# First expert products of two chunks worked as a pair, the half-filled fifth matmuls as two 64-row tiles of the array

## The chip, the cores and the metric

The kernel runs on one core of a Trainium2 chip. The metric is the device time of one execution in microseconds (us); the time before is the median of three runs. A profile of one execution gives each instruction's start and duration. TensorE is called PE in its rows, its weight loads PEld, VectorE DVE, ScalarE ACT, GpSimd POOL and the queue that issues most DMAs SP.

## The reference

One block of a vision model on a map of 192 channels by 128 by 128 positions, in fp32. First a channel attention (1x1 convolution, 3x3 depthwise convolution, attention over channels, projection) with a residual. Then the part that is changed, a mixture of four experts over the 16384 positions as tokens:

```python
scores = jnp.einsum('bsd,de->bse', x, gate_w) + gate_b
probs = jax.nn.softmax(scores, axis=-1)
topk_vals, topk_idx = jax.lax.top_k(probs, TOP_K)          # TOP_K = 2 of 4 experts
...
h = jax.nn.gelu(jnp.einsum('bsd,edh->ebsh', x, w1) + b1[:, None, None, :], approximate=False)
y = jnp.einsum('ebsh,ehd->ebsd', h, w2) + b2[:, None, None, :]
out = jnp.einsum('bse,ebsd->bsd', masked, y)
```

A token has 192 numbers, the hidden layer of an expert 768.

## The kernel before

The first phase of the program (the `p1` block) does the normalisation, both convolutions and the products of the attention. The second (`p2`) projects, routes the tokens, and works the experts; at the end the result is transposed and written. All engines are programmed by hand, each with its own loop over "beats", and meet by semaphores. The order on every engine is therefore the order of the code.

Tokens that chose the same expert are scattered into lists in DRAM and read back in blocks of 512 (`TOK`). There are 67 blocks (`NJ`), one to a beat. A block has six chunks (`CH`) of 128 hidden units, so there are 402 chunks. Within a beat, for block `J` and chunk `k`:

- PE, `first(J, k)`: the hidden units of chunk `k` for 512 tokens, into one of the two banks `lb`, bank `k % 2`.
- ACT, `chunk`: Gelu out of the bank into `hf`, then a rounded copy `hh`. DVE: the rest, `hl = hf - hh`.
- PE, `second(J, k - LAG)`, two chunks later (`LAG` is 2): four token tiles of 128, each one matmul with `hh` (384 columns) and one with `hl` (192 columns), summed over the chunks in the four banks `yb`. The last two chunks of a block are worked in the next beat.
- PE, `turn`: eight transposes bring the next block's tokens (`xs`) into two banks `mb`; ACT and DVE split them into high and low parts. Every few beats `project` follows at the end of the beat (16 matmuls), for the stage before the experts.
- DVE, `expert_out(J)`: for each of the four tiles `upper` (first half of the bank times the gate weight, plus bias) and `lower` (second half added). `second(J, 0)` may overwrite tile `t` of `yb` when `lower(t)` of the block before is done. POOL then adds the tile to DRAM with an indirect DMA.

Accuracy is kept by splitting each factor into a rounded high part and a low rest, held as fp32r. A token has 192 numbers where the array has 128 rows. So `first` takes three full matmuls for the first 128 numbers (high x high, low weights x high, high weights x low), and for the last 64 the two halves of the rows are used for two things: `x_c` holds the high parts in rows 0 to 63 and the low parts in rows 64 to 127. The fourth matmul (weights quarter 2, the high weights in both halves) gives high x high and high x low at once. The fifth (quarter 3, the low weights in both halves) is needed only for low weights x high parts, that is for half of its rows.

## Time and profile before

| what | value |
|---|---|
| time, median of 3 runs (lowest, highest) | 1994.67 us (1994.42, 1999.99) |
| span of the profiled execution | 1993.4 us |
| the execution's time beside its span | not given apart; the median lies 1.3 us above the span |
| TensorE busy in the span | 1838.7 us (92%) |
| VectorE, ScalarE, GpSimd busy | 1379.8 (69%), 1277.2 (64%), 1123.5 (56%) |
| DMA, mean over the span | 182 GB/s |
| first matmul of the experts, last one of `second` | 834 us, 1906 us |

The span goes from the first to the last instruction. A busy time is the union of an engine's instructions; those of TensorE overlap, since a matmul's recorded duration reaches to its last result while the next one is already streaming. What a matmul takes of the engine is the distance from its start to the next start.

### The profile page before, as it was taken

To read this page: it belongs to the slowest core of one execution; us is meant where nothing else is said; L and a number is where in the kernel's file an instruction comes from. 1 tells how busy PE (TensorE), PEld (TensorE's weight loads), DVE (VectorE), ACT (ScalarE), POOL (GpSimd) and SP (SyncE) were. 2 spreads that over 40 slices of the span, in tenths; PEclk is the share of its full clock that TensorE was granted. 3 is DMA by queue.
4 is the path that set the end of the run, shared out by engine and by line. 5 is a ranking of instruction groups with operands and counts; after the bars stand their busy time and mean duration, and the time that the engine had idled before them with its cause. 6 is when DMAs were issued, how large, how long until landed. Compare 5 with 4: busy or idle time off the path is not lost.

```text
span 1993.4 us, 36026 instructions
## 1 busy us (share of the span) xinstructions
PE 1838.7 (92%) x9782; PEld 1502.9 (75%) x9782; DVE 1379.8 (69%) x3382; ACT 1277.2 (64%) x2468; POOL 1123.5 (56%) x1079
## 2 busy tenths in 40 slices
PE   5799999999795989898999999999999999999956
PEld 3566666666564767688989989899898888888844
DVE  3789999999777474667676686776766655555532
ACT  3688888888674435465666666666667667676622
POOL 3666666666663015476767676767677676344320
PEclk9899999999896999899999999999999999999977
DMA  3453323333333798777788878788787877656569
GB/s 97 147 148 93 92 89 93 92 91 92 99 111 95 228 290 275 263 221 216 211 229 215 227 213 228 213 229 224 216 226 195 242 204 202 171 155 180 129 184 338
DMA packets 254367, 361.97 MB, mean 182 GB/s; under 512 B 27396, under 2 KB 183940, under 8 KB 254212
## 3 DMA queue, kind: packets, MB, share of 16 engines
q1 hardware_dynamic: 191556, 278.59, 46.3%
q0 software_dynamic: 50880, 60.59, 15.0%
q10 hardware_dynamic: 11776, 20.98, 3.0%
q8 instruction: 67, 1.10, 0.2%
q14 instruction: 88, 0.72, 0.1%
HBM read 222.76 MB, written 137.30 MB: 181 GB/s over the span
## 4 chain that ended last, share of the span: by engine, by line
PE 57%; DMA 4%; DVE 3%; POOL 2%; issue 2%; ACT 1%; SPq 1%; POOLq 0%; DVEq 0%; ACTq 0%
PE bank L1804 21%; PE bank L1820 14%; PE bank L1787 7%; PE bank L1821 6%; PE bank L1847 4%; DMA xn<-acc_scratch 3%; PE bank L1839 3%; POOL xs_scratch L1251 1%; POOL acc_scratch L1266 1%; PE bank L1869 1%; DMA acc_scratch<-yo,tix 1%; DMA xs<-xs_scratch 0%; PE bank L1872 0%; DVE hl L1758 0%; ACT L1319 0%
## 5 line engine op out<-in xcount | busy, mean ns | idle before, releaser
L1266 POOL DMA_INDIRECT acc_scratch<-yo,tix x268 | 439.0, 1638 | 304.2 <-DVE yo L1647 238.0
L1804 PE MATMUL bank<-x_all,w1b 128*128 128x512 f32 x2010 | 548.8, 402 | 1.0 <-ACT hf L1319 1.0
L1820 PE MATMUL bank<-w_hl,hh 128*128 x1608 | 495.5, 360 | 6.7 <-DVE hl L1758 5.8
L1319 ACT ACTIVATE hf<-bank,b_col 128x512 f32<-128x512 f32 x402 | 276.7, 688 | 335.5 <-PE bank L1804 335.4
L1758 DVE TENSOR_TENSOR hl<-hf,hh 128x512 fp32r<-128x512 f32 x402 | 277.2, 690 | 272.5 <-ACT hh L1322 272.3
L1821 PE MATMUL bank<-w_hl,hl 128*128 x1608 | 404.9, 252 | 0.0
L1804 PEld LDWEIGHTS bank<-x_all,w1b 128*128 128x128 f32 x2010 | 348.2, 188 | 55.1 <-ACT hf L1319 1.4
L625 DVE SCALAR_TENSOR_TENSOR bank<-zwin,wdw,bank 128x512 f32<-128x512 f32 (+2 forms) x462 | 336.3, 734 | 43.4 <-PE bank L731 34.8
L1820 PEld LDWEIGHTS bank<-w_hl,hh 128*128 128x128 f32 x1608 | 302.1, 188 | 40.9 <-issue 10.4
L1821 PEld LDWEIGHTS bank<-w_hl,hl 128*128 128x128 f32 x1608 | 306.1, 190 | 17.4
L1251 POOL DMA_INDIRECT xs_scratch<-xn,idx x256 | 262.2, 1024 | 85.1 <-issue 75.7
L1322 ACT ACTIVATE hh<-hf 128x512 fp32r<-128x512 f32 x402 | 253.9, 632 | 12.7
L429 POOL TENSOR_TENSOR last_tap<-acc,last_tap 128x512 f32<-128x512 f32 (+2 forms) x99 | 125.5, 1268 | 181.6 <-ACT last_tap L495 146.0
L731 PE MATMUL bank<-zwin,diag 128*128 128x512 f32 (+2 forms) x462 | 213.8, 592 | 3.4 <-DVE acc L625 3.4
L731 PEld LDWEIGHTS bank<-zwin,diag 128*128 128x128 f32 x462 | 83.6, 194 | 69.7 <-issue 61.1
L1787 PE MATMUL bank<-x_all,w1b 120*96 120x512 f32 x381 | 123.8, 423 | 6.7 <-issue 3.7
L432 POOL TENSOR_TENSOR qs<-last_tap,s_bc 128x512 f32<-128x512 f32 (+2 forms) x99 | 124.1, 1254 | 7.8
L1642 DVE SCALAR_TENSOR_TENSOR yo<-bank,wt,b2w 128x192 f32<-128x192 f32 x268 | 104.4, 410 | 30.1 <-PE bank L1821 30.0
L1329 ACT ACTIVATE b2w<-b2b,wt 128x192 f32 x268 | 118.1, 441 | 0.0
L1647 DVE SCALAR_TENSOR_TENSOR yo<-bank,wt,yo 128x192 f32<-128x192 f32 x268 | 103.7, 407 | 0.0
L1847 PE MATMUL bank<-mt,vd 96*128 96x200 f32 (+1 forms) x512 | 98.3, 346 | 5.7 <-DMA vd<-u_scratch 3.5
L479 ACT ACTIVATE zwin<-bank,bz 128x512 f32<-128x512 f32 x96 | 66.1, 688 | 58.4 <-PE bank L773 58.4
(261 smaller groups left out, 2902.3 us busy)
## 6 DMA issues: line engine op xcount, KB each, us to landing
w1b<-w1s_scratch SPq DMA_DIRECT2D x134, 768.0 KB, 5.1
xs<-xs_scratch SPq DMA_DIRECT2D x67, 522.0 KB, 6.0
xtok_scratch<-xtok SPq DMA_DIRECT2D x32, 384.0 KB, 2.7
v_scratch<-zv SPq DMA_DIRECT2D x64, 192.0 KB
vc_scratch<-yo ACTq DMA_DIRECT2D x64, 192.0 KB, 4.5
vd<-vc_scratch SPq DMA_DIRECT2D x64, 192.0 KB
xtok<-xtok_scratch SPq DMA_DIRECT2D x32, 384.0 KB, 7.3
acc_scratch<-x SPq DMA_DIRECT2D x32, 384.0 KB, 5.5
```

What stands on the lines that cost most here:

```text
L625: nc.vector.scalar_tensor_tensor(out=acc[:, ct, lo:hi, :] if last else bank, in0=zwin[n.par][:, ct, ky + lo:ky + hi, kx:kx + W], scalar=wd ...
L731: last = nc.tensor.matmul(db[(n.par + ct) % 2][:, lo * W:hi * W].rearrange("p (r w) -> p r w", w=W), diag[:, ct, k, :], zwin[n.par][:, ct, ...
L1251: nc.gpsimd.indirect_dma_start(xs_dram, bass.IndirectOffsetOnAxis(ap=idx[:, h, b * NT + t:b * NT + t + 1], axis=0), src, None).then_inc(st ...
L1266: nc.gpsimd.indirect_dma_start(acc_dram, bass.IndirectOffsetOnAxis(ap=tix[:, J % 4, t:t + 1], axis=0), yo[:, J % YN, t, :], None, compute_ ...
L1319: nc.scalar.activation(hf[:, k % 3, :], lb[k % 2][:, :], ACT.Gelu, bias=b1_col[:, bass.ds(exp_of[J] * CH + k, 1)]).then_inc(gelu, 1)
L1322: nc.scalar.activation(hh[:, k % 3, :], hf[:, k % 3, :], ACT.Copy).then_inc(hh_ok, 1)
L1758: nc.vector.tensor_tensor(hl[:, k % 3, :], hf[:, k % 3, :], hh[:, k % 3, :].bitcast(FP32), ALU.subtract).then_inc(hl_ok, 1)
L1787: last = nc.tensor.matmul(cb[u % 4][0:MV, :].rearrange("p (b w) -> p b w", w=W), w[:, kx, :], v[:, :, kx:kx + W], start=(n == 0), stop=(n ...
L1804: last = nc.tensor.matmul(lb[k % 2][:, :], w[:, q, :], v[:, J % 2, :], start=(i == 0), stop=(i == 4))
L1820: nc.tensor.matmul(yb[t][:, 0:2 * C], hh[:, k % 3, cols], w, start=(k == 0), stop=False, skip_group_check=True)
L1821: last = nc.tensor.matmul(yb[t][:, 0:C], hl[:, k % 3, cols], w[:, 0:C], start=False, stop=(k == CH - 1), skip_group_check=True)
L1847: last = nc.tensor.matmul(mb[t // 2][:, t % 2 * CY:t % 2 * CY + CY], vd[0:rows, s % 2, g, t, :], mt[0:rows, g, :], start=(g == 0 and t % 2 ...
```

## The change

In `first_pair(J, k)` the chunks `k` and `k + 1` are worked together, `k` even. Bank 0 gets the four whole matmuls of chunk `k`, then its fifth as a matmul of 64 rows (rows 0 to 63 of the array). Directly behind it comes the fifth of chunk `k + 1` as a matmul of rows 64 to 127, into bank 1, which it opens, and then the four whole ones of chunk `k + 1`. The 64-row matmuls read a new tile `xh_c`, which holds the high parts in both halves. It costs ACT one more copy per block (x_c's upper 64 rows), since `x_c` can't hold both.

Two `second`s follow each pair. The transposes of the next block come after `second(J, 1)` and no longer after `second(J, 0)`; ACT and DVE split them one chunk later. The second half of a block's weights is waited for before chunk 2 and not before chunk 3. `expert_out` is in two halves: tiles 0 and 1 before `hl` of chunk 1, tiles 2 and 3 behind it. Some small tiles are made smaller or share a place, to make room for `xh_c`.

```diff
@@ scalar
-                        if k == 2 and nxt is not None:
+                        if k == 3 and nxt is not None:
...
                             act.wait_ge(ac2, 2 * nxt + 2)
-                            nc.scalar.activation(x_c[:, nxt % 2, :], mb[1][:, :], ACT.Copy).then_inc(hi2, 1)
+                            nc.scalar.activation(xh_c[:, nxt % 2, :], mb[1][:, :], ACT.Copy).then_inc(hi2, 1)
+                            nc.scalar.activation(x_c[0:CB, nxt % 2, :], mb[1][0:CB, :], ACT.Copy).then_inc(hi2, 1)
@@ vector
-                    upper(0)
-                    for t in range(1, ROWS):
+                    for t in tiles:
                         upper(t)
-                        lower(t - 1)
-                    lower(ROWS - 1)
+                    for t in tiles:
+                        lower(t)
...
                         if k == 1 and prev is not None:
-                            expert_out(prev)
-                        if k == 3 and nxt is not None:
+                            expert_out(prev, (0, 1))
+                        if k == 4 and nxt is not None:
...
                             nc.vector.tensor_tensor(hl[:, k % 3, :], hf[:, k % 3, :], hh[:, k % 3, :].bitcast(FP32), ALU.subtract).then_inc(hl_ok, 1)
+                        if k == 1 and prev is not None:
+                            expert_out(prev, (2, 3))
@@ tensor
-                def first(J, k):
+                def first_pair(J, k):
...
-                    if k % 3 == 0:
-                        pe.wait_ge(ld_w1[J % 2][k // 3], 16 * (J // 2 + 1))
+                    if k != 4:
+                        pe.wait_ge(ld_w1[J % 2][k // 2], 16 * (J // 2 + 1))
                     wait(pe, gelu, c - 1)
-                    w = w1b[:, J % 2, k, 0:512].rearrange("p (q n) -> p q n", q=4)
-                    ops = [(0, xh_a), (1, xh_a), (0, xl_a), (2, x_c), (3, x_c)]
-                    for i, (q, v) in enumerate(ops):
-                        last = nc.tensor.matmul(lb[k % 2][:, :], w[:, q, :], v[:, J % 2, :], start=(i == 0), stop=(i == 4))
+                    w = w1b[:, J % 2, k:k + 2, 0:512].rearrange("p m (q n) -> p m q n", q=4)
+                    whole = [(0, xh_a), (1, xh_a), (0, xl_a), (2, x_c)]
+                    for i, (q, v) in enumerate(whole):
+                        nc.tensor.matmul(lb[0][:, :], w[:, 0, q, :], v[:, J % 2, :], start=(i == 0), stop=False)
+                    wait(pe, gelu, c)
+                    nc.tensor.matmul(lb[0][:, :], w[0:CB, 0, 3, :], xh_c[0:CB, J % 2, :], start=False, stop=True).then_inc(l1, 1)
+                    nc.tensor.matmul(lb[1][:, :], w[CB:128, 1, 3, :], xh_c[CB:128, J % 2, :], start=True, stop=False)
+                    for i, (q, v) in enumerate(whole):
+                        last = nc.tensor.matmul(lb[1][:, :], w[:, 1, q, :], v[:, J % 2, :], start=False, stop=(i == 3))
                     last.then_inc(l1, 1)
...
-                    for k in range(CH):
+                    for k in range(0, CH, 2):
                         if J is not None:
-                            first(J, k)
-                        if k < LAG:
-                            if prev is not None:
-                                second(prev, CH - LAG + k)
-                        elif J is not None:
-                            second(J, k - LAG)
+                            first_pair(J, k)
+                        for m in (k, k + 1):
+                            if m < LAG:
+                                if prev is not None:
+                                    second(prev, CH - LAG + m)
+                            elif J is not None:
+                                second(J, m - LAG)
                         if k == 2 and nxt is not None:
                             turn(nxt, n)
```

The order on TensorE from chunk 2's `first` into `second(J, 0)`, before. L1804 is `first`, L1812 reads the block's expert, L1820 and L1821 are the `hh` and `hl` matmuls of `second`:

```order
L1804 MATMUL bank<-x_all,w1b 128x512 x5
L1812 TENSOR_LOAD tab
L1812 ISA x2
L1820 ISA
L1820 MATMUL bank<-w_hl,hh 128x384
L1821 MATMUL bank<-w_hl,hl 128x192
```

The same place after the change. L1805 and L1810 are the whole matmuls of the two chunks, L1807 and L1808 the two of 64 rows (the shape shown is that of the result), L1826 and L1827 stand for `second`:

```order
L1805 MATMUL bank<-x_all,w1b 128x512 x4
L1807 MATMUL bank<-x_all,w1b 128x512
L1808 MATMUL bank<-x_all,w1b 128x512
L1810 MATMUL bank<-x_all,w1b 128x512 x4
L1818 TENSOR_LOAD tab
L1818 ISA x2
L1826 ISA
L1826 MATMUL bank<-w_hl,hh 128x384
L1827 MATMUL bank<-w_hl,hl 128x192
```

The number of matmuls is the same, ten for two chunks. They now stand in one stretch, with the two of 64 rows in its middle, and two `second`s (each four times the last two rows) stand behind one another.

On VectorE, `expert_out` of the block before (L1642 `upper`, L1647 `lower`) among the `hl` of the chunks (L1758), before:

```order
L1758 TENSOR_TENSOR hl<-hf,hh 128x512 x4
L1642 SCALAR_TENSOR_TENSOR yo<-bank,wt,b2w 128x192 x2
L1647 SCALAR_TENSOR_TENSOR yo<-bank,wt,yo 128x192
L1642 SCALAR_TENSOR_TENSOR yo<-bank,wt,b2w 128x192
L1647 SCALAR_TENSOR_TENSOR yo<-bank,wt,yo 128x192
L1642 SCALAR_TENSOR_TENSOR yo<-bank,wt,b2w 128x192
L1647 SCALAR_TENSOR_TENSOR yo<-bank,wt,yo 128x192 x2
L1758 TENSOR_TENSOR hl<-hf,hh 128x512 x2
```

And after, where `hl` is L1757:

```order
L1757 TENSOR_TENSOR hl<-hf,hh 128x512 x3
L1642 SCALAR_TENSOR_TENSOR yo<-bank,wt,b2w 128x192 x2
L1647 SCALAR_TENSOR_TENSOR yo<-bank,wt,yo 128x192 x2
L1757 TENSOR_TENSOR hl<-hf,hh 128x512
L1642 SCALAR_TENSOR_TENSOR yo<-bank,wt,b2w 128x192 x2
L1647 SCALAR_TENSOR_TENSOR yo<-bank,wt,yo 128x192 x2
L1757 TENSOR_TENSOR hl<-hf,hh 128x512 x2
```

The eight operations of `expert_out` are the same; one `hl` now stands between the two halves.

## Rows read from the trace of the kernel before

**Rows 1.** The page's chain that ended last, by engine and by line

```profile
PE 57%; DMA 4%; DVE 3%; POOL 2%; issue 2%; ACT 1%; SPq 1%; POOLq 0%; DVEq 0%; ACTq 0%
PE bank L1804 21%; PE bank L1820 14%; PE bank L1787 7%; PE bank L1821 6%; PE bank L1847 4%; DMA xn<-acc_scratch 3%; PE bank L1839 3%; POOL xs_scratch L1251 1%; POOL acc_scratch L1266 1%; PE bank L1869 1%; DMA acc_scratch<-yo,tix 1%; DMA xs<-xs_scratch 0%; PE bank L1872 0%; DVE hl L1758 0%; ACT L1319 0%
```

**Rows 2.** Busy times by stretch, experts in the second row

```profile
core 0: us, PE busy (x) PEld busy (x) DVE busy (x) ACT busy (x) POOL busy (x), PEclk, DMA share, GB/s
906.00:1906.00 1000.00, 995.80 (x5741) 896.21 (x5740) 656.75 (x1767) 672.46 (x1185) 634.48 (x482) 1.00 0.77 204
```

**Rows 3.** Groups by line, whole span, two of TensorE

```profile
L1804 PE MATMUL bank<-x_all,w1b 128*128 128x512 f32 x2010 | 548.8, 402 | 1.0 <-ACT hf L1319 1.0
L1820 PE MATMUL bank<-w_hl,hh 128*128 x1608 | 495.5, 360 | 6.7 <-DVE hl L1758 5.8
```

**Rows 4.** Timeline of TensorE, a beat's chunks: start, us, what

```profile
1206.45 1.35 PE L1804 MATMUL bank<-x_all,w1b 128*128 128x512 f32 x5
1207.64 0.34 PE L1820 MATMUL bank<-w_hl,hh 128*128 x1
...
1208.76 1.34 PE L1804 MATMUL bank<-x_all,w1b 128*128 128x512 f32 x5
1209.94 0.34 PE L1820 MATMUL bank<-w_hl,hh 128*128 x1
...
1210.20 0.36 PE L1820 MATMUL bank<-w_hl,hh 128*128 x1
1210.40 0.25 PE L1821 MATMUL bank<-w_hl,hl 128*128 x1
1210.59 0.44 PE L1820 MATMUL bank<-w_hl,hh 128*128 x1
1210.87 0.25 PE L1821 MATMUL bank<-w_hl,hl 128*128 x1
```

**Rows 5.** Timeline of TensorE and its weight loads at the first phase's setup

```profile
23.03 0.42 PE L847 MATMUL bank<-ident,wpr 128*96 128x128 f32 x1
23.38 0.34 PE L848 MATMUL bank<-ident,wpr 64*96 64x64 f32 x1
...
22.82 0.20 PEld L847 LDWEIGHTS bank<-ident,wpr 128*96 128x96 f32 x1
23.38 0.15 PEld L848 LDWEIGHTS bank<-ident,wpr 64*96 64x96 f32 x1 [0.36 <-issue]
```

**Rows 6.** Timeline of TensorE around three matmuls of 3 rows, and its clock there

```profile
630.65 3.19 PE L1787 MATMUL bank<-x_all,w1b 120*96 120x512 f32 x7
...
633.21 0.63 PE L1787 MATMUL bank<-x_all,w1b 120*96 120x512 f32 x1
633.77 0.52 PE L1888 MATMUL bank<-rn_row,sel 3*96 3x128 f32 x1
...
633.77 1.59 PE L1888 MATMUL bank<-rn_row,sel 3*96 3x128 f32 x6
...
634.94 0.42 PE L1888 MATMUL bank<-rn_row,sel 3*96 3x128 f32 x1
635.29 0.74 PE L1787 MATMUL bank<-x_all,w1b 120*96 120x512 f32 x1
...
630.00:637.00 7.00, 7.00 (x19) 4.49 (x19) 3.22 (x10) 1.10 (x3) 0.00 (x0) 0.50 0.37 105
```

**Rows 7.** Who waited for whom, 906 to 1900 us: total, times, longest

```profile
ACT hf L1319 <- PE bank L1804: 318.3, 356, 9.8
DVE hl L1758 <- ACT hh L1322: 253.4, 249, 2.5
...
PEld bank L1820 <- DVE yo L1647: 9.1, 52, 0.3
```

**Rows 8.** Timeline of VectorE and ScalarE in the same beat as rows 4

```profile
1208.17 0.74 DVE L1642 SCALAR_TENSOR_TENSOR yo<-bank,wt,b2w 128x192 f32<-128x192 f32 x2 [0.46 <-PE bank L1821]
...
1210.13 0.73 DVE L1647 SCALAR_TENSOR_TENSOR yo<-bank,wt,yo 128x192 f32<-128x192 f32 x2
1210.78 0.68 DVE L1758 TENSOR_TENSOR hl<-hf,hh 128x512 fp32r<-128x512 f32 x1
...
1210.96 0.63 ACT L1322 ACTIVATE hh<-hf 128x512 fp32r<-128x512 f32 x1
1211.50 0.44 ACT L1329 ACTIVATE b2w<-b2b,wt 128x192 f32 x1
1211.93 0.60 ACT L1375 ACTIVATE x_all<-bank 128x512 fp32r<-128x512 f32 x1
1212.42 0.59 ACT L1377 ACTIVATE x_all<-bank 128x512 fp32r<-128x512 f32 x1
1213.64 0.69 ACT L1319 ACTIVATE hf<-bank,b_col 128x512 f32<-128x512 f32 x1 [0.62 <-PE bank L1804]
```

**Rows 9.** `project` on TensorE: a timeline row, and the group by line

```profile
1201.43 2.90 PE L1847 MATMUL bank<-mt,vd 96*128 96x200 f32 x16
...
L1847 PE MATMUL bank<-mt,vd 96*128 96x200 f32 (+1 forms) x300 | 54.5, 334 | 0.0
```

More of the change, by code:

```diff
@@ L941, in build @@
             rcol = sb(p2, "rcol", [128, 8, NT])
-            tri = sb(p2, "tri", [128, NT, E, E])
+            tri = sb(p2, "tri", [128, E, E])
             msk = sb(p2, "msk", [128, NT, E])
@@ L953, in build @@
             tokid = sb(p2, "tokid", [128, NB * ROWS])
-            tok_i = sb(p2, "tok_i", [128, NB * ROWS], mybir.dt.int32)
+            tok_i = idx[:, 0, :].bitcast(mybir.dt.int32)
             tab = sb(p2, "tab", [128, NG, 2, MAXB], mybir.dt.int32)
@@ L974, in build @@
             xs = sb(p2, "xs", [128, 2, ROWS, CW])
-            x_all = sb(p2, "x_all", [128, 3, 2, TOK], F32R)
-            xh_a, xl_a, x_c = (x_all[:, k, :, :] for k in range(3))
-            zl_c = sb(p2, "zl_c", [128, 4, W + 2], F32R)
+            x_all = sb(p2, "x_all", [128, 4, 2, TOK], F32R)
+            xh_a, xl_a, x_c, xh_c = (x_all[:, k, :, :] for k in range(4))
             hf = sb(p2, "hf", [128, 3, TOK])
@@ L1006, in build @@
             z_hi = [window(x_all, n * ZW, KV, 4, W + 2) for n in range(3)]
-            z_lo = [window(x_all, (3 + n) * ZW, KV, 4, W + 2) for n in range(2)] + [zl_c[0:KV, :, :]]
+            z_lo = [window(x_all, (3 + n) * ZW, KV, 4, W + 2) for n in range(2)] + [window(x_all, 6 * TOK, KV, 4, W + 2)]
             band_place = [(w1b, n * BW) for n in range(21)] + [(t, n * BW) for t in (hh, hl) for n in range(5)] + [(x_all, 5 * ZW)]
@@ L1217, in _ @@
                 nc.gpsimd.memset(zrow[:, :, :], 0.0).then_inc(c2, 1)
-                nc.gpsimd.memset(tri[:, :, :, :], 1.0).then_inc(c2, 1)
+                nc.gpsimd.memset(tri[:, :, :], 1.0).then_inc(c2, 1)
                 nc.gpsimd.memset(tri_s[:, :], 1.0).then_inc(c2, 1)
@@ L1228, in _ @@
                 pool.wait_ge(c2, 11)
-                nc.gpsimd.affine_select(out=tri[:, :, :, :], in_=tri[:, :, :, :], compare_op=ALU.is_gt, fill=0.0,
-                                        base=0, pattern=[[0, NT], [1, E], [-1, E]], channel_multiplier=0).then_inc(c2, 1)
+                nc.gpsimd.affine_select(out=tri[:, :, :], in_=tri[:, :, :], compare_op=ALU.is_gt, fill=0.0,
+                                        base=0, pattern=[[1, E], [-1, E]], channel_multiplier=0).then_inc(c2, 1)
                 nc.gpsimd.affine_select(out=tri_s[:, :], in_=tri_s[:, :], compare_op=ALU.is_gt, fill=0.0,
@@ L1487, in gate @@
                     linked()
-                    link(nc.vector.tensor_tensor(cmp_[:, 2], cmp_[:, 1], tri[:, :, :, :], ALU.mult))
+                    link(nc.vector.tensor_tensor(cmp_[:, 2], cmp_[:, 1], tri[:, None, :, :].to_broadcast([128, NT, E, E]), ALU.mult))
                     yield
@@ L1630, in meta, with expert_out @@
                     nc.vector.tensor_copy(tix[:, J % 4, :], xs[:, J % 2, :, CID]).then_inc(meta_ok, 1)
-                def expert_out(J):
-                    if J >= YN:
+                def expert_out(J, tiles):
+                    if tiles[0] == 0 and J >= YN:
                         added(dve, J - YN)
-                    if J == 0:
+                    if J == 0 and tiles[0] == 0:
                         stored(dve, UNITS)
@@ L1744, in _ @@
                         if k == 1 and prev is not None:
-                            expert_out(prev)
-                        if k == 3 and nxt is not None:
+                            expert_out(prev, (0, 1))
+                        if k == 4 and nxt is not None:
                             if J is None:
                                 some(places, 99)
-                            dve.wait_ge(hi2, 2 * nxt + 2)
+                            dve.wait_ge(hi2, 3 * nxt + 3)
                             nc.vector.tensor_tensor(xl_a[:, nxt % 2, :], mb[0][:, :], xh_a[:, nxt % 2, :].bitcast(FP32), ALU.subtract).then_inc(lo2, 1)
-                            nc.vector.tensor_tensor(x_c[CB:128, nxt % 2, :], mb[1][CB:128, :], x_c[CB:128, nxt % 2, :].bitcast(FP32), ALU.subtract)\
+                            nc.vector.tensor_tensor(x_c[CB:128, nxt % 2, :], mb[1][CB:128, :], xh_c[CB:128, nxt % 2, :].bitcast(FP32), ALU.subtract)\
                                 .then_inc(lo2, 1)
```

## The prediction

> **What bounds the kernel now.** I began with the chain that ended last [rows 1]: 57% of the span is TensorE's, and the lines of the experts (L1804, L1820, L1821, L1839) make up most of that. The busy times by stretch then say how tight this stage is [rows 2]: in 1000 us of the experts TensorE is busy for 995.80, at a granted clock of 1.00, while VectorE has 656.75, ScalarE 672.46 and GpSimd 634.48. The waits confirm it [rows 7]: ScalarE waited 318.3 us for the results of `first`, VectorE 253.4 us for ScalarE, and TensorE's only wait of size is 9.1 us in 52 places for `lower` (L1647), which frees the banks of `second`. So what TensorE spends from start to start in this stage is the time of the stage, and each microsecond added to or taken from it counts nearly whole.
>
> From start to start, five matmuls of `first` take 1207.64 - 1206.45 = 1.19 us and 1209.94 - 1208.76 = 1.18 us [rows 4]. One of 512 columns thus takes 0.24 us. The recorded mean of 402 ns [rows 3] is its latency and not its price.
>
> **The change part by part.** There are 67 blocks of six chunks, 402 chunks, 201 pairs; 2010 matmuls of `first` [rows 3] agree (402 x 5).
>
> *The fifth matmuls.* The two 64-row matmuls lie in different rows of the array and go to different banks. If they stream side by side, a pair saves one slot: 0.24 us, and 201 x 0.24 = 48 us in all. Against it stand two changes of the number of rows, 128 to 64 and back to 128, in each pair. The price of such a change is the whole question, and two places of this trace show it.
>
> At the setup a matmul of 128 rows is followed by one of 64 [rows 5]. In a stream the next weights are loaded while the matmul before is at work: L847's load begins at 22.82, its matmul only at 23.03. The load of L848, the 64-row one, begins at 23.38, after 0.36 us of idle time that no other engine ended, and at the same moment as its own matmul. Neither the load ahead nor the overlap of two matmuls is there across the change.
>
> The second place gives sizes, at the half clock (0.50, 1.2 GHz) [rows 6]. Seven matmuls of 120 rows by 512 columns take 3.19 us, the last of them 0.63: (3.19 - 0.63) / 6 = 0.43 us from start to start. The last one starts at 633.21 and the first of 3 rows at 633.77, 0.56 us on: 0.13 more than the 0.43. On the way back, 634.94 to 635.29 is 0.35 us, where these matmuls otherwise take (1.59 - 0.42) / 5 = 0.23: 0.12 more. And the first matmul after it lasts 0.74 instead of 0.63, since its weights were not yet there: 0.11 more. One change costs 0.13 of draining and 0.11 of an uncovered load, 0.24 us.
>
> That is at the half clock, and the experts run at the full one. The uncovered load has a row there: where `second` had waited for VectorE, its matmul and its load began together at 1210.59, it lasted 0.44 instead of 0.36, and the next start came 0.28 later where 0.20 is usual (1210.20 to 1210.40) [rows 4]: 0.08 us. The draining has no row at the full clock. Its bounds are 0.065 (all of it cycles of the array, half of 0.13) and 0.13 (none of it). I take the middle, 0.10, so that a change costs 0.18 us, with 0.145 and 0.21 as bounds. The half-clock rows are for 3 rows and not for 64, but the setup shows the same signature for 64.
>
> A price of nothing for the change can't be read from these rows. Matmuls of 96 and of 100 rows do alternate in `project` without any such stop, (2.90 - 0.33) / 15 = 0.17 us from start to start [rows 9]. So not every change of the row count costs; one down to 64 did in rows 5.
>
> *The second tile behind the first.* Its load can't lie under a whole matmul as others do. It lies between nothing (it is loaded together with the first one's) and an uncovered 0.08. I take 0.04.
>
> The sum for a pair: 2 x 0.18 + 0.04 - 0.24 = +0.16 us, and 201 x 0.16 = +32 us. The bounds are 2 x 0.145 + 0 - 0.24 = +0.05 (+10 us) and 2 x 0.21 + 0.08 - 0.24 = +0.26 (+52 us).
>
> The Trainium skill (TensorEngine Tiling, section Key Properties) says the same: a change of the tiling mode, not of the tile alone, drains TensorE. It gives no figure; the rows above do.
>
> *The stall at second(J, 0).* Before, `second(prev, 5)` and `second(J, 0)` are one `first` (1.18 us) apart, and the eight operations of `expert_out` run from 1208.17 to 1210.86 [rows 8], past the start of `second(J, 0)` at 1209.94 [rows 4]. Hence the 9.1 us in 52 waits [rows 7], to which 52 uncovered loads of 0.08 are to be added (4.2 us): 13 us. After the change the two are a whole pair apart, some 2.5 us. `lower` of tiles 2 and 3 then comes later by one `hl` of 0.68 us [rows 8], but is needed later by 1.3 us: `expert_out` starts 0.53 us after `second(prev, 5)` (1208.17, 1207.64), so tile 3 is ready 0.53 + 2.69 + 0.68 = 3.9 us after that start, and its bank is asked for at 1.12 + 2.5 + 3 x 0.28 = 4.5. The stall goes: -13 us. If it stays, nothing.
>
> *Waits that the new order brings.* Bank 0 is asked for at the start of a pair, bank 1 after four matmuls. Bank 1's chunk ended with the pair before, so Gelu has two `second`s (2 x 1.12) and four matmuls (0.95) for it, 3.2 us, where it needs 0.69, and at worst 0.63 of `hh` and 0.44 of a bias copy ahead of it [rows 8]. ScalarE has one more copy per block, at most 0.59 us as L1377's [rows 8]; the three copies follow the transposes, and the next Gelu (chunk 4) is due some 1.2 us after these end. So it may be late by about 0.6 us, but bank 0 is asked for again only in the next beat. The cover is ScalarE's idle share, a third of the stage [rows 2]; without it 67 x 0.6 = 40 us would show. `hl` of the pair's second chunk is needed after a full pair and one `second`, later than before in relation to its `first`. VectorE's splitting of the next block comes one chunk later and ends some 1.5 us ahead of the next beat. The weights' second half is asked for one chunk earlier; it is issued a beat ahead. All of these I cost at nothing. SP's queue keeps its order, and GpSimd's adds follow `lower`, for which POOL waits anyway.
>
> The small tiles of the setup (`tri`, `tok_i`) work on fewer elements or the same, outside the experts: nothing.
>
> Sum: +32 - 13 = +19 us. The profiled span is 1993.4 us and the median 1994.67, 1.3 us above it; the sum is made on the span, and the same 1.3 us lie around it afterwards: 1993.4 + 19 + 1.3 = 2014 us.
>
> **The rivals.**
>
> *The change of rows is cheap at the full clock, and the kernel gets faster.* If TensorE loads the 64-row weights ahead and only drains, at the lower bound, a pair costs 2 x 0.065 - 0.24 = -0.11 us: -22 us, with the stall -35, 1960 us. With no price at all it is -48 - 13 = -61 us, 1934 us. It decides below a price of about 0.13 us a change (2 x 0.13 + 0.04 - 0.24 = +0.06, 12 us, which the stall pays). For it: the half clock may exaggerate, and rows 9 show changes of row count for free. Against it: both places with a small row count show drain and uncovered load, and the uncovered load alone is 0.08 at the full clock. The rule that speaks for it is in the Trainium skill (TensorE: Matmul & The Clock Gate, Part 3): matmuls in different row tiles start about 4 ns apart, and a weight load for other rows overlaps a matmul in flight. Nothing in this trace shows two tiles at work. 13% for 1960, 4% for 1934.
>
> *The two tiles don't stream side by side.* Then the slot is not saved and both switches are paid: 0.24 in place of the 0.04, 201 x 0.20 = 40 us more, 2054 us. For it: the trace has no case of it, and both are fed from one queue in order. Against: different rows, different banks. 15%.
>
> *It cancels.* Both changes at the lower bound, +10, and the stall's -13, give -3 us: 1992 us, no change that a measurement tells (0.3%, 6 us, is what can be told here). 12%.
>
> **How the numbers follow.** The forecast, a real price at the full clock and tiles side by side, has 56%; its own range is 1994.7 + 10 - 13 = 1992 to 1994.7 + 52 = 2047. Slower by over 0.3% holds most of it and the case without overlap: 0.56 + 0.15, less a little at the lower edge, 0.70. Within 0.3%: 0.12. Faster by over 0.3%: 0.17, with the edge 0.18. The range reaches down between the forecast and the cheap switch, to 1976, and up to the case without overlap, 2056.
>
> **What would show it.** In the profile after: the start of the first 64-row matmul should lie about 0.33 to 0.37 us after the last whole one of bank 0 (0.24 in a stream), its weight load beginning with it and not before; the two 64-row starts should be 0.0 to 0.1 us apart (0.24 would mean no overlap); and the first whole one of bank 1 should come 0.3 us or more after them, again with its load uncovered. From the start of a pair to the first matmul of `second` it should be about 2.53 us where twice 1.185 is 2.37. The row of waits for L1647 should be gone. The prediction is wrong if the load of the 64-row weights begins under the whole matmul, if the pair takes under 2.3 us, or if TensorE's idle time in the experts grows, which would point to a wait (for Gelu, or for the split of the next block) and not to the array.

## The result and the profile after

| | time, median | runs | ratio to before (95% interval) |
|---|---|---|---|
| before | 1995.17 us | 6 | |
| after | 2005.25 us | 6 | 1.0046 (1.0032 to 1.006) |

The change makes the kernel 0.46% slower, some 9 to 10 us. Forecast were 19 us more (2014); the measured time lies in the range and has the sign of the forecast, but half its size. The span went from 1993.4 to 2003.5 us.

The busy times by stretch after (columns as in [rows 2]) still show a stage that TensorE fills:

```profile
906.00:1916.00 1010.00, 1009.41 (x5730) 844.18 (x5728) 654.07 (x1758) 682.75 (x1247) 646.77 (x480) 1.00 0.76 201
```

TensorE is now busy for all but 0.6 of 1010 us; before 4.2 of 1000 were idle [rows 2]. Its weight loads (PEld) fell from 896.21 us in 1000 to 844.18 us in 1010: they stand still where the row count changes. The price of that is in the timeline of TensorE, one pair of chunks:

```profile
1208.92 1.10 PE L1805 MATMUL bank<-x_all,w1b 128*128 128x512 f32 x4
1209.95 0.50 PE L1807 MATMUL bank<-x_all,w1b 64*128 64x512 f32 x1
1209.96 0.50 PE L1808 MATMUL bank<-x_all,w1b 64*128 64x512 f32 x1
1210.38 1.19 PE L1810 MATMUL bank<-x_all,w1b 128*128 128x512 f32 x4
1211.42 0.34 PE L1826 MATMUL bank<-w_hl,hh 128*128 x1
```

Its weight loads in the same place:

```profile
1209.95 0.18 PEld L1807 LDWEIGHTS bank<-x_all,w1b 64*128 64x128 f32 x1 [0.35 <-issue]
1209.95 0.18 PEld L1808 LDWEIGHTS bank<-x_all,w1b 64*128 64x128 f32 x1
1210.38 0.76 PEld L1810 LDWEIGHTS bank<-x_all,w1b 128*128 128x128 f32 x4 [0.25 <-issue]
```

The two 64-row matmuls start 0.01 us apart, so they do stream side by side. Their loads begin with them and not under the matmul before, after 0.35 us in which nothing was loaded: the signature of [rows 5]. The pair takes 1211.42 - 1208.92 = 2.50 us where twice 1.185 had been 2.37 (forecast 2.53).

So the signs named in the prediction came: load with the matmul and not before it, tiles side by side, and a gap of 0.43 us to the first whole matmul of bank 1 (1209.95 to 1210.38). The gap from the last whole matmul of bank 0 to the first 64-row one is 0.32 us in the middle of the 200 pairs of this trace, just under the 0.33 to 0.37 forecast.

The three largest waits of TensorE's weight loads in the experts, after (total, times, longest). `PEld ... <- issue` is no other engine's doing:

```profile
PEld bank L1807 <- issue: 71.5, 199, 0.4
PEld bank L1810 <- issue: 48.7, 200, 0.2
PEld bank L1826 <- issue: 4.1, 1, 4.1
```

The wait for `lower` in [rows 7] (9.1 us, 52 times) has no row any more. Of the waits that the new order might have brought, for Gelu before bank 1 (L1807), there is 0.4 us once in the whole stage.

### The profile page after: what moved, and what is told of

The parts are those of the page before. It is cut to its first block, busy times and chain, and to the rows that moved or that the text cites. A ratio compares the mean times of both kernels' runs of the same rounds, so it can differ in the third digit from the quotient of the medians.

```text
span 2003.5 us, 36093 instructions
## 1 busy us (share of the span) xinstructions
PE 1854.7 (93%) x9782; PEld 1449.9 (72%) x9782; DVE 1377.4 (69%) x3382; ACT 1289.4 (64%) x2535; POOL 1137.7 (57%) x1079
## 4 chain that ended last, share of the span: by engine, by line
PE 58%; DMA 4%; DVE 3%; POOL 2%; issue 2%; ACT 1%; SPq 0%; POOLq 0%; DVEq 0%; ACTq 0%
PE bank L1826 14%; PE bank L1810 10%; PE bank L1805 9%; PE bank L1788 7%; PE bank L1827 6%; PE bank L1853 4%; PE bank L1807 4%; DMA xn<-acc_scratch 3%; PE bank L1845 3%; POOL xs_scratch L1250 1%; POOL acc_scratch L1265 1%; DMA acc_scratch<-yo,tix 0%; PE bank L1875 0%; DVE hl L1757 0%; DVE stat L1436 0%
## 5 line engine op out<-in xcount | busy, mean ns | idle before, releaser
L1265 POOL DMA_INDIRECT acc_scratch<-yo,tix x268 | 449.0, 1675 | 300.8 <-DVE yo L1647 216.1
L1826 PE MATMUL bank<-w_hl,hh 128*128 x1608 | 473.2, 359 | 3.9 <-DVE hl L1757 3.9
L1757 DVE TENSOR_TENSOR hl<-hf,hh 128x512 fp32r<-128x512 f32 x402 | 277.3, 690 | 237.3 <-ACT hh L1321 236.9
L1827 PE MATMUL bank<-w_hl,hl 128*128 x1608 | 403.5, 251 | 0.0
L1827 PEld LDWEIGHTS bank<-w_hl,hl 128*128 128x128 f32 x1608 | 307.2, 191 | 8.9
L1826 PEld LDWEIGHTS bank<-w_hl,hh 128*128 128x128 f32 x1608 | 302.7, 188 | 13.3 <-issue 4.1
L1810 PE MATMUL bank<-x_all,w1b 128*128 128x512 f32 x804 | 241.8, 422 | 0.0
L1805 PE MATMUL bank<-x_all,w1b 128*128 128x512 f32 x804 | 229.0, 406 | 1.1 <-ACT hf L1318 1.1
L1810 PEld LDWEIGHTS bank<-x_all,w1b 128*128 128x128 f32 x804 | 135.3, 188 | 67.9 <-issue 48.9
L1805 PEld LDWEIGHTS bank<-x_all,w1b 128*128 128x128 f32 x804 | 137.0, 189 | 18.4 <-issue 1.5
L1788 PE MATMUL bank<-x_all,w1b 120*96 120x512 f32 x444 | 134.7, 413 | 7.7 <-issue 4.5
L1642 DVE SCALAR_TENSOR_TENSOR yo<-bank,wt,b2w 128x192 f32<-128x192 f32 x268 | 99.0, 410 | 27.9 <-PE bank L1827 27.6
```

The source lines that it names most:

```text
L1265: nc.gpsimd.indirect_dma_start(acc_dram, bass.IndirectOffsetOnAxis(ap=tix[:, J % 4, t:t + 1], axis=0), yo[:, J % YN, t, :], None, compute_ ...
L1757: nc.vector.tensor_tensor(hl[:, k % 3, :], hf[:, k % 3, :], hh[:, k % 3, :].bitcast(FP32), ALU.subtract).then_inc(hl_ok, 1)
L1788: last = nc.tensor.matmul(cb[u % 4][0:MV, :].rearrange("p (b w) -> p b w", w=W), w[:, kx, :], v[:, :, kx:kx + W], start=(n == 0), stop=(n ...
L1805: nc.tensor.matmul(lb[0][:, :], w[:, 0, q, :], v[:, J % 2, :], start=(i == 0), stop=False)
L1810: last = nc.tensor.matmul(lb[1][:, :], w[:, 1, q, :], v[:, J % 2, :], start=False, stop=(i == 3))
L1826: nc.tensor.matmul(yb[t][:, 0:2 * C], hh[:, k % 3, cols], w, start=(k == 0), stop=False, skip_group_check=True)
```

## The experiments

Each ratio is to the kernel before, timed beside that run, with its 95% interval. The "stage" is the time from the first start of `first` to the last start of an `hh` matmul of `second`, read from those two lines' rows. It leaves out the phases around it, which vary by a few us from run to run. The time of a part of the stage is summed from start to next start over the trace's matmuls. A "quiet beat" is one without `project` and without routing, from the first transposing matmul to the next beat's.

### Whole matmuls in the place of the tiles (e1)

```diff
-                    nc.tensor.matmul(lb[0][:, :], w[0:CB, 0, 3, :], xh_c[0:CB, J % 2, :], start=False, stop=True).then_inc(l1, 1)
-                    nc.tensor.matmul(lb[1][:, :], w[CB:128, 1, 3, :], xh_c[CB:128, J % 2, :], start=True, stop=False)
+                    nc.tensor.matmul(lb[0][:, :], w[:, 0, 3, :], x_c[:, J % 2, :], start=False, stop=True).then_inc(l1, 1)
+                    nc.tensor.matmul(lb[1][:, :], w[:, 1, 3, :], x_c[:, J % 2, :], start=True, stop=False)
```

> The changed kernel with its two 64-row matmuls made into whole ones of 128 rows again (reading x_c), in the same places; all else of the change stays, the pair order, the later split and the third copy on ScalarE too. The price theory reads from the profile after the change that a pair pays 0.158 us net for the tiles (from the last whole matmul of bank 0 to the second whole one of bank 1 it is 0.319 + 0.003 + 0.428 + 0.340 = 1.090 us where four slots are 0.932). It expects 201 x 0.158 = 32 us less than the changed kernel: about 1973 us, so 22 us under the kernel before. The rival, that what the order gave back hangs on the tiles or that a faster TensorE runs into a wait (a bank of Gelu, the banks of the second products), expects 1985 to 1995 us.

Measured: 1971.99 us, ratio 0.9882 (0.9864 to 0.99). The tiles cost 33 us, and what is left of the change gains 24. The price theory holds on the total. The pair itself shows more than it expected:

```profile
1212.29 1.10 PE L1805 MATMUL bank<-x_all,w1b 128*128 128x512 f32 x4
1213.22 0.39 PE L1807 MATMUL bank<-x_all,w1b 128*128 128x512 f32 x1
1213.45 0.39 PE L1808 MATMUL bank<-x_all,w1b 128*128 128x512 f32 x1
1213.68 1.07 PE L1810 MATMUL bank<-x_all,w1b 128*128 128x512 f32 x4
1214.58 0.34 PE L1826 MATMUL bank<-w_hl,hh 128*128 x1
```

Ten whole matmuls take 1214.58 - 1212.29 = 2.29 us, where the changed kernel's pair took 2.50. That is 0.20 us a pair, and some 38 to 40 us over 201 pairs, not 32. The stage grew by 33.2 us only (1050.1 to 1083.3), because waits behind the pairs shrink when TensorE is slower: the row `PE bank L1865 <- DVE x_all L1750: 2.5, 5, 0.7` of e1 (routing) has no counterpart after the change, and the one wait for `hl` at the start of the stage is 3.9 us in place of 5.3.

### Both 64-row matmuls in rows 0 to 63 (e2)

```diff
-                    nc.tensor.matmul(lb[1][:, :], w[CB:128, 1, 3, :], xh_c[CB:128, J % 2, :], start=True, stop=False)
+                    nc.tensor.matmul(lb[1][:, :], w[0:CB, 1, 3, :], xh_c[0:CB, J % 2, :], start=True, stop=False)
```

> The changed kernel with both 64-row matmuls in rows 0 to 63 of the array, so that they can't stream side by side; the number of changes between 128 and 64 rows stays. If the tiles do overlap in the changed kernel (starts 3 ns apart), and this is worth a slot, this one is 201 x 0.23 = 46 us slower than the changed kernel, about 2051 us. If in addition the second one's weights can't be loaded under the first, it is 0.1 us a pair more, about 2071 us. If the 3 ns are only how the starts are recorded, it takes the same 2005 us.

Measured: 2048.67 us, ratio 1.0263 (1.0246 to 1.028), 43 us more than the changed kernel. Its timeline of TensorE:

```profile
1210.93 1.18 PE L1805 MATMUL bank<-x_all,w1b 128*128 128x512 f32 x4
1212.04 0.49 PE L1807 MATMUL bank<-x_all,w1b 64*128 64x512 f32 x1
1212.37 0.39 PE L1808 MATMUL bank<-x_all,w1b 64*128 64x512 f32 x1
1212.70 1.20 PE L1810 MATMUL bank<-x_all,w1b 128*128 128x512 f32 x4
1213.73 0.34 PE L1826 MATMUL bank<-w_hl,hh 128*128 x1
```

From the first 64-row start to the first whole one it is 0.66 us, with tiles side by side 0.43. The overlap is real and worth a whole slot (the time from one start to the next in a stream, 0.23 us). The rival without overlap (15%) is out.

### The 64-row fifth in the old order (e3)

```diff
-                        last = nc.tensor.matmul(lb[k % 2][:, :], w[:, q, :], v[:, J % 2, :], start=(i == 0), stop=(i == 4))
+                        r = slice(0, CB if i == 4 else 128)
+                        last = nc.tensor.matmul(lb[k % 2][:, :], w[r, q, :], v[r, J % 2, :], start=(i == 0), stop=(i == 4))
```

> The kernel before, in its old order, with the fifth matmul of every chunk on rows 0 to 63 alone (it leaves out the product of the two low parts, which is negligible). Two changes of row count for each of 402 chunks and no second tile. The price theory expects per chunk 0.319 + 0.428 + 0.340 - 3 x 0.233 = 0.39 us, for the half that is followed by a wider second product rather less at its end, so between 402 x 0.3 and 402 x 0.39: 2115 to 2151 us. The rival, that the cost in the changed kernel comes from the change of bank or from two tiles loaded together, expects 1995 us.

Measured: 2117.35 us, ratio 1.0617 (1.0595 to 1.0639), 122 us over the kernel before: the lower end of the 2115 to 2151 expected. Five matmuls now take from 1212.10 to 1213.56, and the first of `second` behind them has its load uncovered (0.45 in place of 0.34, next start 0.28 later):

```profile
1212.10 1.53 PE L1805 MATMUL bank<-x_all,w1b 128*128 128x512 f32 x5
1213.56 0.45 PE L1821 MATMUL bank<-w_hl,hh 128*128 x1
1213.84 0.25 PE L1822 MATMUL bank<-w_hl,hl 128*128 x1
```

1213.84 - 1212.10 = 1.74 us where [rows 4] have 1207.82 - 1206.45 = 1.37 (the start of the `hl` matmul at 1207.82 is 0.18 behind 1207.64). That is 0.37 us for two changes, 402 x 0.37 = 149 us. The stage grew by 125 us (832.1 to 2029.2, 1197.1). The 24 us between the two are about what the kernel before lost to waits that are gone or shorter here: 15.5 us at `second(J, 0)` (see e10), 3.8 for `msk`, and 5 for `hl` at the start of the stage. One matmul of 64 rows among whole ones, in one bank and with no tile beside it, is enough for the price.

### The split of the next block at its old place (e4)

The transposes stand behind `second(J, 0)`, ScalarE's copies in chunk 2, VectorE's split in chunk 3; the fifths are whole.

```diff
-                        if k == 3 and nxt is not None:
+                        if k == 2 and nxt is not None:
                             act.wait_ge(ac2, 2 * nxt + 1)
...
-                        if k == 4 and nxt is not None:
+                        if k == 3 and nxt is not None:
...
-                        if k == 2 and nxt is not None:
-                            turn(nxt, n)
+                            if m == 2 and nxt is not None:
+                                turn(nxt, n)
```

> As e1, with whole fifths in the pair order, but the transposes of the next block again right behind second(J, 0), ScalarE's copies in chunk 2 and VectorE's split in chunk 3, as in the kernel before. The theory that the later split freed VectorE for the routing in time (TensorE's wait of 1.08 us for msk at 1284.41 before the change has no counterpart after it) expects the gate beats to lose about 0.8 to 1.1 us each again, 7 of them: 6 to 8 us over e1. A rival, that the pair order and the halved expert_out did it, expects the same time as e1.

Measured: 1972.63 us, ratio 0.9885 (0.9868 to 0.9901), the same as e1. My theory of the later split falls: with the split at its old place the wait in the routing beats is not longer but gone from the rows of TensorE's matmuls, while the one at the start of the stage is 7.1 us in place of e1's 5.3.

### expert_out in one piece (e5)

```diff
-                    for t in tiles:
-                        upper(t)
-                    for t in tiles:
-                        lower(t)
+                    upper(0)
+                    for t in range(1, ROWS):
+                        upper(t)
+                        lower(t - 1)
+                    lower(ROWS - 1)
...
-                            expert_out(prev, (0, 1))
+                            expert_out(prev, (0, 1, 2, 3))
...
-                        if k == 1 and prev is not None:
-                            expert_out(prev, (2, 3))
```

> As e1 (pair order, whole fifths, 1972 us), but expert_out in one piece again, in the old order of its eight operations, ahead of hl of chunk 1. The theory that the pair order on TensorE alone frees the banks of the second products in time (a pair, now 2.36 us, lies between second(prev, 5) and second(J, 0)) expects the same as e1, 1972 us within 3. The rival, that the halved expert_out is what removed the wait, expects the 52 waits of 0.2 us back: 8 to 13 us more.

Measured: 1972.28 us, ratio 0.9878 (0.9863 to 0.9894). The same as e1.

### Only expert_out in two halves, old order (e6)

The kernel before with the change's `expert_out` and nothing else of it.

> The kernel before with only expert_out in two halves, hl of chunk 1 between them, in the old order on TensorE. The pair-order theory expects it to be slower: lower of tiles 2 and 3 comes 0.7 us later while TensorE asks for the banks as early as before, so the wait at second(J, 0) grows from 0.2 to about 0.8 us in 66 beats: 1995 + 40 = 2035 us, at least 2015. The rival, that the split alone gave back 10 to 20 us, expects 1975 to 1985.

Measured: 2030.37 us, ratio 1.0176 (1.0159 to 1.0192), 34 us slower. Its waits on TensorE:

```profile
PEld bank L1821 <- DVE yo L1647: 48.8, 63, 1.1
PE bank L1821 <- DVE yo L1647: 34.1, 63, 0.9
```

The halved `expert_out` is no part of the gain. It is a cost that the pair order hides (e1 has it and e5 has not, in the same time).

### Two copies in place of three (e7)

```diff
-                            nc.scalar.activation(xh_c[:, nxt % 2, :], mb[1][:, :], ACT.Copy).then_inc(hi2, 1)
-                            nc.scalar.activation(x_c[0:CB, nxt % 2, :], mb[1][0:CB, :], ACT.Copy).then_inc(hi2, 1)
+                            nc.scalar.activation(x_c[:, nxt % 2, :], mb[1][:, :], ACT.Copy).then_inc(hi2, 1)
```

> As e1, but x_c in one copy again and xh_c not written: two ScalarE copies a block in place of three. It is what is left of the change when the tiles go. ScalarE is busy for two thirds of the stage and its copy of 0.59 us lies under TensorE's second products, so the price theory expects e1's time, 1972 us within 3. The rival, that the third copy delays a Gelu (67 x 0.59 = 40 us at most), expects less than 1965.

Measured: 1969.12 us, ratio 0.9867 (0.9847 to 0.9887). The interval overlaps e1's, and the stage is equal to 0.1 us. The third copy costs nothing.

### Fifths of 96 rows (e8)

```diff
-                    nc.tensor.matmul(lb[0][:, :], w[:, 0, 3, :], x_c[:, J % 2, :], start=False, stop=True).then_inc(l1, 1)
-                    nc.tensor.matmul(lb[1][:, :], w[:, 1, 3, :], x_c[:, J % 2, :], start=True, stop=False)
+                    nc.tensor.matmul(lb[0][:, :], w[0:96, 0, 3, :], x_c[0:96, J % 2, :], start=False, stop=True).then_inc(l1, 1)
+                    nc.tensor.matmul(lb[1][:, :], w[0:96, 1, 3, :], x_c[0:96, J % 2, :], start=True, stop=False)
```

> As e1, but both fifths on rows 0 to 95 (x_c, so that the products of rows 96 to 127, low parts with low parts, are left out). In the trace before, matmuls of 96, 100 and 128 rows follow one another without a stop. If the price hangs on the step to 64 rows and not on any change of row count, this is e1's time, 1972 us within 4. If every change of row count costs, it has the two changes per pair without a second tile side by side: about 201 x 0.39 = 78 us more, 2050 us.

Measured: 1976.98 us, ratio 0.9896 (0.9881 to 0.9912). That is 5 us more than e1, 3 of them outside the stage, with intervals that overlap. The stream has no stop:

```profile
1215.80 0.40 PE L1807 MATMUL bank<-x_all,w1b 96*128 96x512 f32 x1
1216.03 0.40 PE L1808 MATMUL bank<-x_all,w1b 96*128 96x512 f32 x1
1216.27 1.09 PE L1810 MATMUL bank<-x_all,w1b 128*128 128x512 f32 x4
```

A step from 128 to 96 rows costs at most 2 us in 201 pairs (0.01 us each), where one to 64 and back costs 0.39.

### Two pairs of tiles behind one change of rows (e9)

The two 64-row matmuls are issued twice in a row.

> The changed kernel with the two 64-row matmuls issued twice in a row, so that two pairs of tiles stand between one change to 64 rows and one back (the product of low weights and high parts is added twice). The price theory says that the cost sits in the two changes and not in the tiles: the second pair of tiles streams behind the first and adds one slot of 0.23 us per pair of chunks, 201 x 0.23 = 46 us over the changed kernel, about 2051 us, with its weights loaded under the first pair. If the two loads of the second pair stand uncovered too, it is 0.1 us more per pair of chunks, 2072 us. If tiles that follow one another in 64-row mode drained as well, 2090 us.

Measured: 2051.46 us, ratio 1.0278 (1.0262 to 1.0293), 46 us over the changed kernel. The timeline of TensorE and the weight loads:

```profile
1214.68 0.49 PE L1807 MATMUL bank<-x_all,w1b 64*128 64x512 f32 x1
1214.68 0.49 PE L1808 MATMUL bank<-x_all,w1b 64*128 64x512 f32 x1
1215.02 0.39 PE L1809 MATMUL bank<-x_all,w1b 64*128 64x512 f32 x1
1215.02 0.39 PE L1810 MATMUL bank<-x_all,w1b 64*128 64x512 f32 x1
1215.34 1.19 PE L1812 MATMUL bank<-x_all,w1b 128*128 128x512 f32 x4
...
1214.79 0.19 PEld L1809 LDWEIGHTS bank<-x_all,w1b 64*128 64x128 f32 x1
```

The second pair's weights are loaded under the first (1214.79, their matmul at 1215.02), and it adds one slot, 0.66 in place of 0.43 us. The cost sits in the two changes, not in the number of tiles between them.

### The order on TensorE alone (e10)

```diff
-                    for k in range(CH):
+                    for k in range(0, CH, 2):
                         if J is not None:
                             first(J, k)
-                        if k < LAG:
-                            if prev is not None:
-                                second(prev, CH - LAG + k)
-                        elif J is not None:
-                            second(J, k - LAG)
-                        if k == 2 and nxt is not None:
-                            turn(nxt, n)
+                            first(J, k + 1)
+                        for m in (k, k + 1):
+                            if m < LAG:
+                                if prev is not None:
+                                    second(prev, CH - LAG + m)
+                            elif J is not None:
+                                second(J, m - LAG)
+                            if m == 2 and nxt is not None:
+                                turn(nxt, n)
```

> The kernel before with one edit: on TensorE the first products of two chunks stand together and two second products behind them; the transposes stay behind second(J, 0). No 64-row matmul, no third copy, no later split, expert_out in one piece. As e4, e5 and e7 each undid one of the other edits and stayed within 4 us of e1, the theory that the order on TensorE alone gives the gain expects 1970 to 1973 us, 0.988 of before. The rival, that the other edits back one another up and all gone together let a wait return, expects 1980 to 1990.

Measured: 1977.19 us, ratio 0.9916 (0.9903 to 0.993). Most of the gain, but 5 to 8 us short of e1 and e7, which neither theory had. The waits for `lower` are gone here too. What they had cost is in the length of `second(J, 0)`, from its first start to the first transposing matmul. Before it begins at 1209.94 [rows 4] and ends with

```profile
1211.29 0.93 PE L1839 MATMUL bank<-ident,xs 128*128 128x128 f32 x7
```

and in e10 it is

```profile
1205.49 0.34 PE L1820 MATMUL bank<-w_hl,hh 128*128 x1
...
1206.62 1.04 PE L1839 MATMUL bank<-ident,xs 128*128 128x128 f32 x8
```

That is 1.35 us before and 1.13 in e10. Over all 67 blocks `second(J, 0)` took 90.9 us before and 75.4 in e10, 15.5 less. The waits for `msk` in the beats with routing fell by 1.3 us in all; before and in e10:

```profile
PE bank L1859 <- DVE msk L1497: 3.8, 5, 0.8
```

```profile
PE bank L1859 <- DVE msk L1497: 2.5, 5, 0.7
```

### What e10 lacks: the order inside a pair? (e11, e12)

In e11 the fifth matmul comes first in odd chunks; in e12 the five stand mirrored.

> The kernel before with the order of e10 on TensorE, and one thing more: in odd chunks the fifth matmul (x_c) comes first and not last, as in e1. e10 has a quiet beat of 14.71 us where e1 has 14.59, 0.08 of it in the first products. If this sits in the order of the matmuls inside the pair (bank 1 opened by x_c), the quiet beat falls to 14.6 and the time to 1969 to 1972 us. If it comes from another edit (the place of the tiles in memory, the third copy, the later split), the time stays at 1977 us.

> As e10, with the five matmuls of each chunk in another order: even chunks xl_a, xh_a, xh_a, x_c, x_c, odd chunks the same backwards. If it is worth something that matmuls which read the same tile stand together and across the change of bank, this is as fast as e11 or faster, 1968 to 1972 us; if not, 1977 us as e10.

Measured: 1977.45 us, ratio 0.9915 (0.9902 to 0.9929), and 1979.34 us, ratio 0.9924 (0.9911 to 0.9938). Neither is faster than e10. The order inside a pair brings nothing.

### What e10 lacks: the place of the tiles in memory (e13, e14, e15)

```diff
-            tri = sb(p2, "tri", [128, NT, E, E])
+            tri = sb(p2, "tri", [128, E, E])
...
-            tok_i = sb(p2, "tok_i", [128, NB * ROWS], mybir.dt.int32)
+            tok_i = idx[:, 0, :].bitcast(mybir.dt.int32)
...
-            x_all = sb(p2, "x_all", [128, 3, 2, TOK], F32R)
+            x_all = sb(p2, "x_all", [128, 4, 2, TOK], F32R)
...
-            zl_c = sb(p2, "zl_c", [128, 4, W + 2], F32R)
```

e13 and e14 have all four of these, e15 the first two alone. `zl_c` becomes a window on the longer `x_all`.

> The kernel before with only the change's edits of memory: tri without its tile dimension (read by broadcast), tok_i in the place of idx, x_all a tile longer (unused but for zl_c's window), so that x_all lies 1472 bytes lower and the tiles behind it 544 bytes higher. If the place of the tiles is what is missing in e10, the quiet beat falls by about 0.1 us from 14.91 and the time is 5 to 8 us under the kernel before, 1988 to 1991 us. If not, it is the same as before.

> e10 (the order on TensorE alone, 1977 us) with the memory edits of e13. If the place of the tiles is the missing part, it reaches e1's and e7's time, 1969 to 1972 us, with a quiet beat of 14.59; else 1977.

> e10 with only the smaller tri and tok_i, which puts x_all and all behind it 1472 bytes lower. If the address of x_all (the tile that the first products stream) matters, it is as fast as e14, 1969 to 1972; if the tiles behind x_all matter or its length, 1977 as e10.

Measured: e13 1993.46 us, ratio 0.9985 (0.9976 to 0.9993); e14 1970.12 us, ratio 0.9872 (0.9856 to 0.9888); e15 1976.02 us, ratio 0.9898 (0.9882 to 0.9915). So the memory edits are what e10 lacked: with them the order alone reaches e1's and e7's time. In the old order they bring 2.5 us (1.4 to 4.8 by the interval) and half a us of the stage (834.5 to 1906.1), so the 5 to 8 us expected of e13 did not come: their worth hangs on the pair order. The ten `first` matmuls of a pair in e14, and then in e10, are the same instructions in the same order:

```profile
1651.49 2.46 PE L1803 MATMUL bank<-x_all,w1b 128*128 128x512 f32 x10
```

```profile
1652.47 2.51 PE L1804 MATMUL bank<-x_all,w1b 128*128 128x512 f32 x10
```

A quiet beat follows, from the transposes' starts, e14 and then e10:

```profile
1640.30 1.04 PE L1838 MATMUL bank<-ident,xs 128*128 128x128 f32 x8
1654.91 1.04 PE L1838 MATMUL bank<-ident,xs 128*128 128x128 f32 x8
```

```profile
1645.85 1.04 PE L1839 MATMUL bank<-ident,xs 128*128 128x128 f32 x8
1660.56 1.04 PE L1839 MATMUL bank<-ident,xs 128*128 128x128 f32 x8
```

14.61 against 14.71 us, 67 x 0.10 = 7 us. e15's stage (833.8 to 1888.0, 1054.2 us) is 2.8 us under e10's 1057.0, less than half of the way to e14's 1050.3, and its time has an interval that overlaps e10's. So which of the tiles matters, x_all or those behind it, stays open.

## Why the prediction had the sign and half the size

Where the stage begins and ends is in the rows of the two lines (count, durations, first and last start). Of the changed kernel they read:

```profile
L1805 PE MATMUL bank<-x_all,w1b x804: 387/396/540, 831.9 to 1909.1; 128*128 128x512 f32 x161
...
L1826 PE MATMUL bank<-w_hl,hh x1608: 338/362/683, 838.4 to 1915.2; 128*128 x179
```

1915.2 - 831.9 = 1083.3 us. The same reading of every kernel gives the account:

| kernel | stage, us | step | us |
|---|---|---|---|
| before | 834.4 to 1906.5: 1072.1 | | |
| e10, order alone | 832.0 to 1889.0: 1057.0 | order | -15.1 |
| e14, order and memory | 831.2 to 1881.5: 1050.3 | memory, given the order | -6.7 |
| e1, all but the tiles | 833.7 to 1883.8: 1050.1 | copy, later split, halves | -0.2 |
| after | 831.9 to 1915.2: 1083.3 | tiles | +33.2 |
| | | sum | +11.2 |

The rest of the span (its start and end) is 1.1 us shorter, which makes the 10.1 of the two spans. The steps add up by construction, each being the difference of two neighbours, and what a part is worth depends on its place in the list: memory alone, in the old order, is 0.5 us of the stage (e13).

- **Tiles: forecast +32, measured +33, in part by luck.** The mechanism and its two sizes were right. By the starts of e2, where the steps can be told apart, the last whole matmul to the first 64-row one and the way back are about 0.09 us longer than a slot each, and each uncovered load costs 0.1 (L1807 to L1808 0.33 where a slot is 0.23). The estimate for draining at the full clock, 0.10 between the bounds 0.065 and 0.13, and the 0.08 of the uncovered load from [rows 4] were each within 0.02. ([rows 6], from which the draining came, show six matmuls of 3 rows, not three.) But against whole matmuls in the same places a pair costs 0.20 us and not 0.16, and the 5 us or more that this makes were given back by waits that the prediction had no term for (e1).
- **The second tile: forecast 0.04, measured under 0.01.** The Trainium skill (TensorE: Matmul & The Clock Gate, Part 3) gives about 4 ns between the starts of such tiles, and the trace agrees: 3 ns. What decided the case was the other rule, the drain on a change of tiling mode (the Trainium skill, TensorEngine Tiling, Key Properties), which every run with a 64-row matmul among whole ones shows (0.09 us longer than a slot in e2).
- **The stall at `second(J, 0)`: forecast -13, measured -15.1 for the order.** The mechanism was right, the term too small. It priced 52 waits with one uncovered load of 0.08 us each; but `second(J, 0)` lost 0.23 us in each of the 67 blocks, 15.5 us: the wait (1210.40 to 1210.59, 0.10 over the usual), the load behind it (0.08) and the next start late once more (1210.96 to 1211.20, 0.04). I had also read only that row of the waits. The one for `msk` gave 1.3 us more, and small increases elsewhere took 1.7 back.
- **Edits at nothing.** The third copy, the later split, the weights asked for earlier and the halves of `expert_out` cost nothing within the pair order (e4, e5, e7). e6 names the price of the last one's cover: 34 us where TensorE asks for the banks at once.
- **The step that failed** is the sentence "The small tiles of the setup (`tri`, `tok_i`) work on fewer elements or the same, outside the experts: nothing". I costed the work in those tiles and not their place. Making room for `xh_c` moved `x_all` and what lies behind it, and with the pair order that is worth 6.7 us (e10 to e14). With the 2.1 us of the stall term it is the 9 us between the 19 forecast and the 10 measured; the tiles' 1.2 us too much and the 1.1 outside the stage cancel. In e14 most of the ten `first` matmuls of a pair start 0.227 us apart, in e10 by turns 0.231 and 0.236 (medians over the pairs). Why the place matters is not shown: no wait has a row for it, only the starts lie closer. Nor is it shown how much of the 6.7 us the changed kernel itself has, since no run has its tiles with the memory as before. In its trace the whole matmuls ahead of the 64-row ones start 0.227 us apart, those behind them 0.235.

The order and the memory edits were each run alone (e10, e13), the tiles were left out alone (e1). The change joined an edit that loses 33 us to one that gains 22; e14, which keeps only the second, is the better kernel by 1.3% on the kernel before.

## What to carry to other kernels

- A half-filled matmul in a stream of whole ones isn't improved by halving the array for it: in these runs the step to 64 rows and back cost 0.39 us at a granted clock of 1.00, and a pair of tiles side by side saved 0.23. By these two numbers (an estimate; no run has it) it pays from two pairs of tiles between the steps on, if these are work that would have taken whole slots; e9 shows that a second pair adds one slot and no further step.
- Work two stretches of the same kind together when a wait sits behind them: the pair order moved the demand for the banks by one stretch, without an engine doing less. Price such a wait by how much longer its stretch takes (1.35 in place of 1.13 us), not by the wait's row, which had 9.1 of the 15.5 us.
- When a large change comes out near nothing, run it with each part undone. Also count the place of tiles among the parts.

## What the runs showed of the hardware that I had not expected

- The same ten matmuls take 2.46 or 2.51 us by where the tiles lie in memory, at a granted clock of 1.00 in both and without a wait. In the old order the same memory edits were worth 2.5 us of time (1.4 to 4.8), half a us of the stage.
- Matmuls of 96 rows among ones of 128 stop nothing (e8: starts 0.23 us apart, a load always ahead); the step lies between 96 and 64.
- In 64-row mode weights are loaded ahead as usual (e9, 1214.79 for 1215.02); it is the step into and out of it that stops the loads (0.35 and 0.25 us without one, after).
